# Staged keys and queries are turned by F32R products with an identity, not by F32 transposes

## The reference

```
q, k, v = split(x @ w_qkv)              # 16 heads of 16
q = q * cos + rotate_half(q) * sin;     k likewise
att = softmax(where(causal, q @ k.T / 4, min))
x = layernorm(x + (att @ v) @ w_proj)
```

## Time and profile before

| | |
|---|---|
| median of three runs | 957.93 us |
| the profiled execution | 960.31 us |
| its span, first to last instruction | 958.6 us |
| mean granted TensorE clock | 0.956 of 2.4 GHz |
| PE busy | 881.7 us, 92% |
| DVE busy | 507.0 us, 53% |
| ACT busy | 377.2 us, 39% |
| POOL busy | 313.2 us, 33% |

### The profile page before, as it was taken

The page is one execution under the profiler, slowest core; times in us unless marked ns, Lnnn a source line. Parts: engine busy times, 40 slices in busy tenths (PEclk is TensorE's granted clock), DMA queues, the critical chain, the costliest instruction groups (busy, mean ns, idle before and its releaser), DMA issues.

```text
span 958.6 us, 14238 instructions
## 1 busy us (share of the span) xinstructions
PE 881.7 (92%) x5034; PEld 579.7 (60%) x5034; DVE 507.0 (53%) x1363; ACT 377.2 (39%) x790; POOL 313.2 (33%) x553
## 2 busy tenths in 40 slices
PE   5789999899999999988989899999999999999996
PEld 2544444346666777876666644443476667887885
DVE  4597888526565632165343678883366653116113
ACT  0566666673334311132111166666633343122210
POOL 4403224236101534344222223223440024335332
PEclk9956999989999999999989989998999999999999
DMA  9800533330000322323222033340000000000000
GB/s 310 333 1 3 186 124 133 123 130 1 1 2 1 104 95 92 128 100 121 88 88 88 13 122 133 134 155 2 1 2 1 1 1 1 1 1 23 1 1 24
DMA packets 23896, 68.71 MB, mean 72 GB/s; under 512 B 4400, under 2 KB 11568, under 8 KB 23600
## 3 DMA queue, kind: packets, MB, share of 16 engines
q1 hardware_dynamic: 23824, 67.77, 20.0%
HBM read 65.40 MB, written 13.63 MB: 82 GB/s over the span
## 4 chain that ended last, share of the span: by engine, by line
PE 76%; DVE 13%; issue 4%; ACT 3%; POOL 3%; SPq 1%; DMA 0%; POOLq 0%; DVEq 0%; ACTq 0%
PE bank L834 24%; PE bank L662 7%; PE bank L644 7%; PE bank L613 6%; PE bank L822 4%; PE bank L743 4%; DVE max_raw L1144 4%; PE bank L753 4%; DVE bank L1146 4%; PE bank L831 3%; PE bank L599 3%; PE bank L694 3%; PE bank L557 2%; PE bank L764 2%; PE bank L711 1%
## 5 line engine op out<-in xcount | busy, mean ns | idle before, releaser
L974 ACT ACTIVATE prob_s<-bank 128x512 f32<-128x512 f32 (+3 forms) x384 | 163.5, 497 | 80.3 <-PE bank L644 79.7
L1428 POOL TENSOR_TENSOR hid_lo_s<-act_raw_s,hid_hi_s 128x512 fp32r<-128x512 f32 x96 | 123.7, 1289 | 215.1 <-DVE hid_hi_s L1298 180.3
L613 PE MATMUL bank<-k_t_s,q_t_s 64*128 64x512 f32 (+3 forms) x384 | 141.1, 465 | 26.3 <-DVE max_raw L1146 15.3
L1298 DVE CAST hid_hi_s<-act_raw_s 128x512 fp32r<-128x512 f32 x64 | 30.5, 477 | 195.4 <-ACT act_raw_s L1035 195.1
L1146 DVE CUSTOM_DVE_ANT_0 bank<-bank,causal_bf 128x128 f32<-128x128 f32 (+3 forms) x256 | 122.8, 511 | 18.9 <-PE bank L613 16.8
L1399 POOL TENSOR_SCALAR_AFFINE_SELECT prob_s<-prob_s 128x128 f32<-128x128 f32 x256 | 72.0, 295 | 166.8 <-ACT prob_s L974 163.5
L644 PE MATMUL bank<-q_t_s,k_t_s 64*128 64x512 f32 (+3 forms) x384 | 115.2, 408 | 2.5 <-issue 1.6
L1035 ACT ACTIVATE act_raw_s<-bank,scales 128x512 f32<-128x512 f32 x64 | 43.7, 688 | 183.6 <-PE bank L834 183.6
L613 PEld LDWEIGHTS bank<-k_t_s,q_t_s 64*128 64x128 f32 x384 | 64.9, 205 | 70.2 <-DVE max_raw L1146 30.7
L644 PEld LDWEIGHTS bank<-q_t_s,k_t_s 64*128 64x128 f32 x384 | 58.5, 195 | 76.1 <-ACT prob_s L974 51.9
L1144 DVE TENSOR_REDUCE max_raw<-bank 128x1 f32<-128x512 f32 x128 | 82.4, 685 | 37.2 <-PE bank L613 37.2
(11 more groups left out here) (154 smaller groups left out, 1516.1 us busy)
## 6 DMA issues: line engine op xcount, KB each, us to landing
ring_s<-scratch SPq DMA_DIRECT2D x34, 512.0 KB, 3.3
home_s<-scratch SPq DMA_DIRECT2D x22, 512.0 KB, 6.0
checked_s<-in_w_ffn SPq DMA_DIRECT2D x2, 3584.0 KB, 17.8
scratch<-in_w_ffn SPq DMA_DIRECT2D x2, 2560.0 KB, 10.6
ring_moved_s<-scratch SPq DMA_DIRECT2D x10, 512.0 KB, 3.1
checked_s<-in_w_ffn SPq DMA_DIRECT2D x1, 4096.0 KB, 32.2
x_t_s<-in_x_t SPq DMA_DIRECT2D x2, 1024.0 KB, 5.5
x_tok_s<-in_x SPq DMA_DIRECT2D x2, 1024.0 KB, 9.3
```

The source lines that it names most:

```text
L613: mm(out[:, 0:k1 - k0], qkt(q, p, 0)[r, P * qt:P * (qt + 1)], qkt(q, p, 1)[r, k0:k1], start=True, stop=True).then_inc(S["max_mm"], 1)
L974: act.activation(prob[q][4 * (s % 2) + j][:, 0:n], S_BANK[j][:, 0:n], ACT.Exp, scale=SCALE).then_inc(S["exp_done"], 1)
L1428: pt(dst[1][:, m], act_raw[q][r % 3][:], dst[0][:, m].bitcast(F32), ALU.subtract).then_inc(S["f_lo"], 1)
```

## The change

A second identity, `ident_r`, of type F32R is added (512 bytes in each partition). ScalarE writes it at the head of its program by a copy of `ident`. TensorE waits for it once, before the first round of `turn`. In every round the four `pe.transpose` of F32 views become four plain matmuls of the F32R stage tile with `ident_r`, each starting and ending its own accumulation. The other transposes of the kernel stay.

```diff
+        ident_r = sb("ident_r", [P, P], F32R)
...
-        for n in "check_act check_op flag_mm flag_set".split():
+        for n in "ident_split check_act check_op flag_mm flag_set".split():
...
         def turn(q, p, i):
 
+            if q == p == i == 0:
+                pe.wait_ge(S["ident_split"], 1)
             if i == 0:
                 wait(pe, q, "stage_hi", 2 * (p + 1))
                 wait(pe, q, "stage_lo", 2 * (p + 1))
             out = use_round(q, ("turn", p, i))
-            st = stage[q][i // 2][:].bitcast(F32)
+            st = stage[q][i // 2][:]
             for j in range(4):
                 t = 4 * (i % 2) + j
-                m = pe.transpose(out[:, P * j:P * (j + 1)], st[:, 2 * t:2 * t + 2].rearrange("p h a e -> p (h a e)"), ident[:])
+                m = mm(out[:, P * j:P * (j + 1)], st[:, 2 * t:2 * t + 2].rearrange("p h a e -> p (h a e)"), L["ident_r"][:], start=True, stop=True)
             m.then_inc(S["round_mm"], 1)
...
         act.wait_ge(set_pool, 11)
+        act.activation(L["ident_r"][:], ident[:], ACT.Copy).then_inc(S["ident_split"], 1)
         for t in range(NT + V_LAG):
             projections(0, t)
```

More of the change, by code:

```diff
@@ L373, in decoder_layer @@
             check_in=check_in, checked=checked, cos_t=cos_t, ctx_t=ctx_t, hid=hid, home=home,
-            home_in=home_in, ident=ident, ident_bf=ident_bf, kx_blocks=kx_blocks, kx_f=kx_f, kx_hl=kx_hl, no_key=no_key, low_any=low_any, low_halves=low_halves, low_sums=low_sums,
+            home_in=home_in, ident=ident, ident_bf=ident_bf, ident_r=ident_r, kx_blocks=kx_blocks, kx_f=kx_f, kx_hl=kx_hl, no_key=no_key, low_any=low_any, low_halves=low_halves, low_sums=low_sums,
             low_max=low_max, mask_in=mask_in, max_raw=max_raw, max_rows=max_rows, max_split=max_split, mean_var=mean_var,
```

## The result

The changed kernel took 968.48 us (median of five runs, 964.82 to 972.66) against 960.59 us of the kernel before (five runs, 957.48 to 961.47): ratio **1.0094**, 95% interval 1.0062 to 1.0125. It is slower by 0.9%, 8 to 9 us (the medians lie 7.9 us apart). The forecast was 958.6 us where the kernel before took 957.93, no measurable change. In a second set of twelve runs the ratio was 1.0088 (1.0049 to 1.0127).

The account below looks back on a forecast made before the run. PE was taken as the bound, with 76% of the chain; +0.015 us a round at 2.4 GHz and +0.03 at 1.2 GHz gave 1.2 us, 0.6 on the path, +0.7: 958.6 us, 8-in-10 range 954.5 to 963.5.

Parts of the forecast that it names:

- The forecast sum: Each round of line 599 at 2.4 GHz: first load +0.05, spacings +0.01, last product -0.045 us; ends -0.03 and +0.04.
- The spacing: Within a round, products start 0.113 us apart against the transposes' 0.111; three spacings add +0.01 us.
- halving the column time buys nothing: In each round at 2.4 GHz the load, not the array's columns, sets the pace.
- The length of the record: Line 599's product records were to be 217 to 231 ns, against a transpose's median of 273 ns.
- The edits beside it: ScalarE's identity copy with its table load (1.7 us in 27.00 us idle) and PE's added wait cost nothing.
- +3.1 us: Upper end of the sum over all rounds: +0.04 us x 78, with all on the path.
- Rival 5: Rounds get cheaper, first load pulled ahead and short products pay: -0.03 to -0.06 x 78 us, 954 to 956 us; 5%.
- The sum that gave +0.7 us: 50 rounds x 0.015 plus 14 rounds at 1.2 GHz x 0.03 make 1.2 us, 0.6 of it on the path.
- as many stretches at 1.2 GHz as now, give or take one or two: Expected sign over the whole kernel: the number of half-clock stretches stays about the same.
- Rival 2: Ahead of step 0 in sequence 1, thinner array work makes the clock fall three more times, 963.7 us; 10%.
- the signs that were to show the forecast wrong: A round under 0.55 or over 0.75 us, or a granted clock of 2.4 GHz from 44 to 89 us.
- Rival 1: From 44.4 to 88.8 us products hold PE at 2.4 GHz: 955.1 us, 935 at the very most; 8%.

Follow-up runs that it names:

- e1_head: The changed kernel with the 256 transposes put back; F32R identity, ScalarE's copy and TensorE's wait stay. Ratio 0.9992 to the kernel before, median 959.87 us.
- e8: Narrow products (128 moving columns) only in the 38 rounds of steps 0 and later, transposes ahead of step 0. Ratio 1.0104 to the kernel before, median 969.59 us.
- e9: Products of 256 moving columns in the 38 rounds of steps 0 and later, transposes ahead of step 0. Ratio 0.9997 to the kernel before, median 959.67 us.
- e3: The changed kernel with every product 256 columns wide, identity beside a zero block. Ratio 1.0026 to the kernel before, median 961.51 us.
- e2: The changed kernel itself again, no edit, twelve runs. Ratio 1.0088 to the kernel before, median 966.83 us.
- e12: Products of 512 moving columns in the rounds of steps 0 and later, transposes ahead of step 0. Ratio 1.0135 to the kernel before, median 974.71 us.
- e11: Narrow products only in the 26 rounds ahead of step 0, transposes in steps 0 and later. Ratio 0.9972 to the kernel before, median 957.46 us.
- e13: Narrow products only in the 26 rounds ahead of step 0, a repeated measurement of that kernel. Ratio 0.9992 to the kernel before, median 958.98 us.
- e4: Narrow products in sequence 0 only (32 rounds), transposes in sequence 1. Ratio 0.9986 to the kernel before, median 965.93 us.

## Why the prediction was wrong

**The round, step by step.** The forecast sum was +0.015 us a round at 2.4 GHz. Measured is 0.59 against 0.58 us from the first start to the next product: within the sum's ends. The spacing behind it was taken right: a round of 0.66 us with a first record of some 0.33 and a last of 0.28 leaves about 0.11. That halving the column time buys nothing held: the rounds of 128 columns have the transposes' spacing. The length of the record was wrong: 217 to 231 ns was forecast, 277 measured. The trace shows why at 418.81 us, where a round follows products of the same shape and takes 0.56 us: its first record is 222 ns long, the second 277 but begins only 0.07 us after the first, while the later ones begin 0.11 us apart. So the longer record begins some 0.05 us early, and the likely reason is that it takes in a wait for its own load of 192 ns.

**The edits beside it** cost nothing, as said. ScalarE's table load moved to the start and its copy took 0.31 us:

```profile
0.78 1.28 ACT L1069 ACT_TABLE_LOAD   x1 [0.78 <-PEq L1548]
4.41 0.31 ACT L1069 ACTIVATE ident_r<-ident 128x128 fp32r<-128x128 f32 x1 [2.35 <-POOL causal_bf L1487]
27.21 0.38 ACT L956 ACTIVATE v_sb_s<-bank 128x256 f32<-128x256 f32 x1 [22.49 <-PE bank L567]
```

e1_head confirms it in twelve runs.

**The sum's small slips.** The upper end of the forecast's own range, 961.7, adds the +3.1 us to 958.6; from 957.93, where its lower end is counted from, it is 961.0. Rival 5 by its own terms reaches down to 953.2, not 954. Neither matters for a result 5 us above the whole range.

**What failed is the clock.** The sum that gave +0.7 us has no term for it: the forecast put the change of the granted clock at nothing, "as many stretches at 1.2 GHz as now, give or take one or two". The runs showed a mean clock of 0.9377 instead of 0.9565, and this is where the loss lies. Rival 2, "the clock falls more often", is what happened, and it had 10%; its price, 963.7 us, also fell short of 968.48. Its mechanism, that a product uses the array's columns for half of a transpose's time and so thins the work, fits e8 against e9 and e3 against e2, where more columns bring the clock back; e12 shows that it is not the whole account. None of the signs that were to show the forecast wrong appeared: a round is 0.66 us, and the clock around 44 to 89 us is half as before (0.58 from 37 to 94 us, where before has 0.61). They watched the round and the first stretch, and not how often the clock falls in the steps. Two of rival 2's terms were mis-sized and one was misplaced:

- The amount. It had three more stretches of 3.4 us at 1.2 GHz, 10 us. The clock's mean fell by 0.9565 - 0.9377 = 0.0188; at half speed that is 0.0188 x 960 / 0.5 = 36 us.
- The price. It had 0.5 us lost for each us at half speed. The mean time rose by 9.8 us (970.1 over e2's twelve runs against 960.3 over 35), 9.8 / 36 = 0.27. Over the ten and 34 runs that the ratio compares it is 7.9 us for 29, again 0.27. Presumably part of the time at half speed lies where other engines bound the kernel; no run measures that.
- The place. It had the steps ahead of step 0 in sequence 1, because the trace showed PE waiting there. e8, e11 and e13 put it into the steps 0 and later. The stretch was also mislabelled: it was to run from 461 to 573 us, but the first score product of sequence 1 starts at 551.17 us, so its end, with the very stretch at 1.2 GHz that gave the price (566.7 to 573.4 us), already lies in the steps 0 and later. Another row was there: from 88.8 to 204 us the clock was 0.97 and not 1.00, so falls already happened inside the steps, and 38 of the 64 rounds lie in such steps.

Rival 1 had it that products might hold the clock where transposes don't. They lower it. The Trainium skill's page "TensorE: Matmul & The Clock Gate", Part 4, says that transposes do not count as PE-busy in the same way; by that the change should have raised the clock, and here it went from 0.9565 to 0.9377. The measurement decides: in these rounds a transpose keeps the clock up about as well as an F32R product of 256 columns (0.9565 against e3's 0.955, 0.9554 against e9's 0.957, each in its own set), and better than one of 128.

That the clock accounts for the whole loss, as far as the runs can tell, is seen at equal clock. Over the 35 runs of the kernel before, a line through time and mean clock falls by 5.8 us for each 0.01; over e2's twelve runs by 5.7. At a clock of 0.95 the two lines give 964.1 us for before and 963.1 us for the change. At equal clock the changed kernel is not slower at all; single runs lie about 1 us off these lines.

## What to carry to other kernels

Where TensorE is the bound and its clock falls now and then, an edit that gives it fewer columns to take in without making the round shorter can cost more than it saves, as here 0.9%: compare mean granted clocks over many runs, not the busy rows of one profile. Before halving an instruction's array time, see what sets its spacing; here the spacing of 0.11 us stayed, no time was gained, and the mean clock fell by 0.019. Where a trace shows clock falls inside a stage that is edited, as here 0.97 over the steps of sequence 0, a change of the clock needs a term in the sum, and a lower clock more than the 10% of a rival.

## What the runs showed of the hardware that was not expected

- The time of one and the same kernel follows its mean granted clock closely: 953.2 us at 0.968 and 964.8 us at 0.948 are both the kernel before, 5.8 us for 0.01.
- 38 rounds of four products move the mean clock from 0.957 to 0.940 and the time by 1%, when each product has 128 columns instead of 256, a difference of some 0.06 us (277 against 217 ns).
- Products of 256 moving columns cost little more than those of 128 behind loads of the same length: 0.73 against 0.66 us for a round of four.
- One kernel's runs can fall into two groups with nothing between: e4's twelve took up to 960.2 us at clocks of 0.956 and over, or from 964.9 us at 0.944 and under. What decides between them is not shown.
